# A six-stage decoder on one core: the constants of the last layers signalled in two parts, and ScalarE's copy of the second batch's first rows put ahead of the first rectifications

## The chip, the cores and the metric

The kernel runs on one core of one Trainium2 chip, in one launch. The metric is the time of one execution on the device in microseconds (us), the lower the better; a number given for a kernel is the median of several executions. The profiler records one execution apart from these.

The engines have short names in what follows: PE is TensorE (matrix products), ACT is ScalarE, DVE is VectorE, POOL is GpSimd, SP is SyncE (here it only issues transfers).

## The reference, cut to what matters

Eight batches of 256 rows with 256 columns pass through six layers. The change lies in the fourth, at its very start:

```python
x = _layernorm(x + _L0_attn_ref(...))      # attention over 16 heads
x = _layernorm(x + _L0_xattn_ref(...))     # attention over the context
x = _layernorm(x + _L0_ffn_ref(...))       # 8 experts, the best 2 of each row
x = _layernorm(x + _L1_attn_ref(...))      # gated attention and an MLP: the change is here
x = _layernorm(x + _L1_xattn_ref(...))
x = _layernorm(x + _L1_ffn_ref(...))

def _L1_attn_ref(x, ...):
    xn = _layernorm(x, ln1_g, ln1_b)
    q, k, v = l2norm(xn @ Wq), l2norm(xn @ Wk), xn @ Wv
    clock = softplus(xn @ clock_w + clock_b)
    gj = -softplus(xn @ gate_w + gate_b)
    gcp = exp(clip(cumsum(gj), -60, 50))
    p = xn @ p_w + p_b
    p_exp = exp(p - max(p)) * clock
    q = rope(q) * gcp / (cumsum(p_exp) + 1e-8)
    k = rope(k) / (gcp + 1e-8) * p_exp
    out = softmax(causal(q k^T / sqrt(Dh))) @ v @ out_w + out_b
    ...                                    # residual, layer norm, MLP with gelu
```

The cumulative sums run along the 256 rows of a batch, so a batch's gates, clocks and p have to be there whole before its scores.

## The kernel before, in words

The first three layers run as phases of their own and end at about 743 us of the span. The last three layers (the function the diff touches) then work on the eight batches in four groups of two batches (`G` groups, `GB` = 2 batches each). A group has four row tiles of 128 rows (`NT` = 4): tiles 0 and 1 are its first batch, tiles 2 and 3 its second (`HALF` = 2). The four groups pass through a pipeline of periods, with one group in its gated attention, the one before it in the rest of that layer, and one in the last layers. Before the pipeline is full there is a prologue for group 0 alone, done batch by batch. The change touches this prologue.

Each engine has its own program, written out in code in the order in which it runs; engines meet at semaphores. No planner or scheduler moves anything. The prologue's steps, with the names and lines of the kernel:

- POOL `gather(0)` (L1488) fetches the experts' results by eight indirect transfers; DVE `combine` (L2619) adds them to x. DVE `front_half` takes the statistics of a batch's two tiles, POOL `front_rstd` (L1532) raises them to a power, DVE `front_rows_of` (L2777) normalises tile by tile (`n3.normed` counts the tiles).
- ACT `front_rows(g, b)` (L2240) scales a normalised tile into `xn`, for two tiles of batch b (`n4.normed` counts). PE `turn` (L1640) transposes the two tiles into a bank, ACT `front_turned` (L2201) copies them out with gain and bias into `xnt`.
- PE `first_form(b, i)` (L1631), i from 0 to 5, forms the six products of a batch (two parts each of gate, clock and p) in two banks in turn. Form i waits until ACT has read form i-2 (`fmread`). ACT reads forms 0 to 3 in `first_rectified` (L2309 a Relu, L2310 an Abs, which signals `fmread`) and forms 4 and 5 in `first_p_rows` (L2316).
- ACT builds the softplus of gates and clocks from exponentials and logarithms (L2327, L2330, L2331, L2334, L2335), whose bias operands are the constants `ones` and `tiny`. DVE's scans (L2799, L2828) make the cumulative sums.
- PE `queries_keys` and `values` (L1631 too) make q, k and v; ACT `square` (L2266) and `value_copy` (L2271) read them. `value_copy` writes into `va`, which must have been filled with 0 and 1 before.

POOL fills the constants in `constants()`: `ones`, `tiny`, `mask1`, `maskx` and a column of `x5t` (L1500 to L1504). Then it waits until DVE has normalised all four tiles (`n3.normed` at `NT`), clears `va` (L1506), drains, writes a column of ones into it (L1508), cuts the two masks to triangles (L1509, L1511), drains again, and signals all of it by one semaphore, `const`.

Who waits for `const`: ACT, ahead of `first_forms(0)`; DVE, ahead of `first_gate(0)`; PE, ahead of `values(0, 0)`.

ACT's order in the prologue is: `front_rows(0, 0)`, `front_turned(0, 0)`, the wait for `const`, `first_forms(0)`, `front_turned(0, 1)`, `first_rows(0)`, and so on. Inside `first_forms(0)`, after the rectifications of forms 0 and 1, stands `front_rows(0, 1)`: the copy of the second batch's tiles. PE's order is: transposes of batch 0, forms 0 and 1 of batch 0, transposes of batch 1 (they need that copy), forms 2 to 5 of batch 0, and then `queries_keys` and `values`.

Of the kernel before, what the change touches and what calls it, by code (L numbers as in the profile page):

```python
# [45 lines left out]
class Memory:  # L46
# [14 lines left out]
    def sem(self, name):  # L61

        s = self.free.pop() if self.free else self.ctx.enter_context(self.nc.semaphore(name))
        self.used.append(s)
        return s
# [1233 lines left out]
def last_layers(nc, dram, memory, keep):  # L1299


    with ExitStack() as ctx:
# [3 lines left out]
        sem = memory.sem  # L1306
# [51 lines left out]
        lastxr, lastxk, lastrl, lastrs = (cut(gating, 1024 * i, dims) for i, dims in enumerate(((KD, GT), (KD, GT), (KD, GT), (NT, D))))  # L1358

        early, rows = keep["early"], keep["rows"]  # L1360
        weights, loaded, const, stored = (sem(f"l_{n}") for n in ("weights", "loaded", "const", "stored"))
        backed = [sem(f"backed{n}") for n in range(2 * NT)]
        fmm, fmread, qkmm, sqd, vmm, vcop = (sem(n) for n in ("fmm", "fmread", "qkmm", "sqd", "vmm", "vcop"))
        lgate, clr, gcr, ginv, uready, clogged, pmaxed, pexp, sumr, lsum, qsum, qfr, kfr = (sem(n) for n in (
# [29 lines left out]
        def x(g, t):  # L1394

            return keep["x"][:, NT * g + t, :]
# [9 lines left out]
        def batch(b):  # L1406

            return slice(b * S, (b + 1) * S)
# [5 lines left out]
        def tiles_of(b):  # L1414

            return slice(0, NT) if b is None else slice(HALF * b, HALF * b + HALF)

        def front_count(g, b):

            return 2 * g + (b or 0) + 1 if g < 2 else g + 3  # L1420
# [9 lines left out]
        def squares_of(g):  # L1430

            return (NT + 1) * g + 1 if g else 0

        def qk_bank(g, t):

            return (FIRSTQK if g == 0 else QKBANK)[t]
# [44 lines left out]
        def _(pool):  # L1481
# [16 lines left out]
            def constants():  # L1498

                pool.memset(ones[:, :], 1.0)  # L1500
                pool.memset(tiny[:, :], 1e-8)
                pool.memset(mask1[:, :], 3e38)
                pool.memset(maskx[:, :], 0.0)
                pool.memset(x5t[:, :, :, 0:1], 0.0)  # L1504
                pool.wait_ge(n3.normed, NT)
                pool.memset(va[:, :, :, :], 0.0)  # L1506
                pool.drain()
                pool.memset(va[:, :, :, DH1:DH1 + 1], 1.0)  # L1508
                pool.affine_select(out=mask1[:, :], in_=mask1[:, :], compare_op=ALU.is_ge,  # L1509
                                   fill=-1e30, base=0, pattern=[[1, P]], channel_multiplier=-1)  # L1510
                pool.affine_select(out=maskx[:, :], in_=maskx[:, :], compare_op=ALU.is_ge, fill=-8e13, base=0,  # L1511
                                   pattern=[[-1, S2]], channel_multiplier=1)
                pool.drain()
                pool.nop().then_inc(const, 1)
# [19 lines left out]
            front_rstd(0, 0)  # L1534
            front_rstd(0, 1)
            constants()
            pool.wait_ge(rows, NR * 16)
            for b in range(GB):
# [647 lines left out]
        def _(act):  # L2186
# [48 lines left out]
            def front_rows(g, b=None):  # L2235

                for t in range(NT)[tiles_of(b)]:
                    act.wait_ge(n3.rstd, front_count(g, t // HALF))
                    act.wait_ge(n3.normed, NT * g + t + 1)
                    act.activation(xn[:, t, :], x(g, t), ACT.Copy, scale=n4.inv[:, t:t + 1]).then_inc(n4.normed, 1)  # L2240
# [20 lines left out]
            def square(g, t):  # L2261

                act.wait_ge(qkmm, NT * g + t + 1)
                if t >= 2:
                    act.wait_ge(ssready, squares_of(g) + t - 1)
                act.activation((sq if g else firstsq)[:, t % 2, :], bank[qk_bank(g, t)][:, :], ACT.Square).then_inc(sqd, 1)  # L2266

            def value_copy(g, t):

                act.wait_ge(vmm, NT * g + t + 1)  # L2270
                act.activation(va[:, t, :, 0:DH1], bank[4 + t % 2][:, 0:D].rearrange("p (h d) -> p h d", d=DH1),  # L2271
                               ACT.Copy).then_inc(vcop, 1)
# [31 lines left out]
            def first_rectified(b, i, positive, size):  # L2304

                c = FORMS[i]
                bias = cols[:, (BP, BCLK, BGATE)[c // 2], c % 2:c % 2 + 1]
                act.wait_ge(fmm, 6 * b + i + 1)
                act.activation(positive[:, c % 2, batch(b)], bank[4 + i % 2][:, 0:S], ACT.Relu, bias=bias)  # L2309
                act.activation(size[:, c % 2, batch(b)], bank[4 + i % 2][:, 0:S], ACT.Abs, bias=bias).then_inc(fmread, 1)  # L2310

            def first_p_rows(b, i):

                c = FORMS[i]
                act.wait_ge(fmm, 6 * b + i + 1)
                act.activation(pexps[:, c, batch(b)], bank[4 + i % 2][:, 0:S], ACT.Identity, bias=cols[:, BP, c:c + 1]).then_inc(fmread, 1)  # L2316

            def first_forms(b):

                part = batch(b)  # L2320
                first_rectified(b, 0, gsum, gabs)
                first_rectified(b, 1, gsum, gabs)
                if b == 0:
                    front_rows(0, 1)
                first_rectified(b, 2, csum, cabs)
                act.drain()
                act.activation(gabs[:, :, part], gabs[:, :, part], ACT.Exp, scale=-1.0)  # L2327
                first_rectified(b, 3, csum, cabs)
                act.drain()
                act.activation(gabs[:, :, part], gabs[:, :, part], ACT.Ln, bias=ones[:, 0:1]).then_inc(lgate, 1)  # L2330
                act.activation(cabs[:, :, part], cabs[:, :, part], ACT.Exp, scale=-1.0)  # L2331
                first_p_rows(b, 4)
                act.drain()
                act.activation(qfac[:, :, part], cabs[:, :, part], ACT.Identity, bias=ones[:, 0:1])  # L2334
                act.activation(clog[:, :, part], cabs[:, :, part], ACT.Ln, bias=ones[:, 0:1]).then_inc(uready, 1)  # L2335
                first_p_rows(b, 5)

            def first_rows(b):

                square(0, HALF * b)  # L2340
                value_copy(0, HALF * b)
                value_copy(0, HALF * b + 1)
                act.wait_ge(pmaxed, b + 1)
                for c in range(KD):
                    last = act.activation(pexps[:, c, batch(b)], pexps[:, c, batch(b)], ACT.Exp, bias=pmax[:, GB * c + b:GB * c + b + 1])
                last.then_inc(pexp, 1)
                square(0, HALF * b + 1)
# [20 lines left out]
                act.wait_ge(qsum, b + 1)  # L2368
                act.activation(qfac[:, :, part], qfac[:, :, part], ACT.Exp, scale=-1.0).then_inc(qfr, 1)

            act.wait_ge(const, 1)
            first_forms(0)
            front_turned(0, 1)
            first_rows(0)
            first_gate(0)
            first_forms(1)
            first_factors(0)
            first_rows(1)
            first_gate(1)
            for j in range(PAIRS1):  # L2380
# [737 lines left out]
def decoder(nc, dram):  # L3118
    with ExitStack() as ctx:
# [28 lines left out]
        memory.free = keep["cleared"]  # L3148
        memory.mark = last
        last_layers(nc, dram, memory, keep)  # L3150


# [59 lines left out]
```

## Time and profile before

| what | value |
|---|---|
| time, median of 3 runs | 1292.72 us (1290.24, 1292.72, 1295.18) |
| the profiled execution's own time | 1288.51 us |
| its span, first to last instruction | 1286.8 us |
| PE busy | 1123.6 us, 87% of the span |
| DVE busy | 743.7 us, 58% |
| ACT busy | 544.2 us, 42% |
| POOL busy | 459.7 us, 36% |
| mean granted TensorE clock | 0.949 of full speed |

The share of PE is an average. In the prologue of the last layers PE is idle for long stretches, and what counts there is the chain of waits between the engines. A row of a timeline gives the start of a piece and its length in us, the engine, the line, what is written and read, how many instructions are merged in it, and in brackets how long the engine had been idle and who ended that. An "x2" piece is two instructions one behind the other. The engine name with a small q (POOLq, ACTq) is that engine's sequencer: drains and waits.

### The profile page before, as it was taken

To read this page: it belongs to the slowest core of one execution; us is meant where nothing else is said; L and a number is where in the kernel's file an instruction comes from. 1 tells how busy PE (TensorE), PEld (TensorE's weight loads), DVE (VectorE), ACT (ScalarE), POOL (GpSimd) and SP (SyncE) were. 2 spreads that over 40 slices of the span, in tenths; PEclk is the share of its full clock that TensorE was granted. 3 is DMA by queue.
4 is the path that set the end of the run, shared out by engine and by line. 5 is a ranking of instruction groups with operands and counts; after the bars stand their busy time and mean duration, and the time that the engine had idled before them with its cause. 6 is when DMAs were issued, how large, how long until landed. Compare 5 with 4: busy or idle time off the path is not lost. (4 is left out here: it accounts for less than half of the span.)

```text
span 1286.8 us, 20425 instructions
## 1 busy us (share of the span) xinstructions
PE 1123.6 (87%) x6750; PEld 796.0 (62%) x6750; DVE 743.7 (58%) x2260; ACT 544.2 (42%) x1407; POOL 459.7 (36%) x539
## 2 busy tenths in 40 slices
PE   7889988998899797799999937788898899789996
PEld 3466455644654576799999924454655575466775
DVE  1473367247534855455555637758748576856366
ACT  1371246125521741333333317466465457543541
POOL 0251025004400784566666541424221522222122
PEclk9999999999999998899999959689998999899999
DMA  5000010020001013741111141101000100000000
GB/s 194 17 1 1 28 46 2 1 56 17 1 1 56 2 55 124 266 145 48 45 50 51 42 141 39 33 1 29 5 8 1 34 9 17 1 1 25 1 1 33
DMA packets 40228, 52.38 MB, mean 41 GB/s; under 512 B 10780, under 2 KB 33372, under 8 KB 40124
## 3 DMA queue, kind: packets, MB, share of 16 engines
q1 hardware_dynamic: 31100, 36.66, 8.8%
q0 software_dynamic: 3408, 9.31, 2.6%
q10 hardware_dynamic: 5616, 5.11, 1.2%
q8 instruction: 55, 0.90, 0.3%
q14 instruction: 49, 0.40, 0.1%
HBM read 41.76 MB, written 9.31 MB: 40 GB/s over the span
## 5 line engine op out<-in xcount | busy, mean ns | idle before, releaser
L1631 PE MATMUL bank<-words 128*128 128x256 f32 (+3 forms) x872 | 276.1, 469 | 26.7 <-DVE words L2639 9.1
L1631 PEld LDWEIGHTS bank<-words 128*128 128x128 f32 (+1 forms) x872 | 166.7, 198 | 112.7 <-issue 58.0
L419 PE MATMUL bank<-words 128*128 128x512 f32 x384 | 171.6, 598 | 8.2 <-DMA words<-in_wq 8.2
L371 POOL TENSOR_TENSOR words<-words 128x256 f32<-128x256 f32 (+1 forms) x128 | 103.6, 831 | 176.3 <-DVE words L972 176.3
L1182 PEld LDWEIGHTS bank<-words 128*128 128x128 f32 x1248 | 147.4, 194 | 3.5 <-ACT words L1216 1.6
L1182 PE MATMUL bank<-words 128*128 128x128 f32 x1248 | 147.9, 277 | 0.9 <-ACT words L1216 0.9
L754 ACT ACTIVATE words<-words 128x128 f32<-128x128 f32 (+1 forms) x256 | 113.3, 444 | 52.8 <-DVE words L967 52.8
L419 PEld LDWEIGHTS bank<-words 128*128 128x128 f32 x384 | 72.1, 192 | 89.5 <-issue 88.9
L706 ACT ACTIVATE words<-bank 128x512 f32<-128x512 f32 x48 | 28.7, 598 | 191.0 <-PE bank L419 191.0
L1231 ACT ACTIVATE words<-words 128x1024 f32 x39 | 41.1, 1057 | 144.4 <-PE bank L1182 127.9
L808 DVE COPY words<-bank 128x512 f32<-128x512 f32 x48 | 33.2, 691 | 104.6 <-PE bank L419 104.3
L963 DVE CUSTOM_DVE_ANT_0 words<-bank,words 128x128 f32<-128x128 f32 (+1 forms) x256 | 76.0, 353 | 21.9 <-PE bank L430 20.6
L1193 PE MATMUL bank<-words 128*128 x312 | 73.9, 380 | 0.7 <-DVE words L1280 0.7
L443 PE MATMUL bank<-words 128*128 128x128 f32 x384 | 56.5, 285 | 16.0 <-POOL words L371 7.5
L430 PE MATMUL bank<-words 64*128 64x128 f32 (+1 forms) x512 | 60.4, 358 | 8.6 <-DVE words L967 5.2
L443 PEld LDWEIGHTS bank<-words 128*128 128x128 f32 x384 | 42.3, 144 | 37.6 <-issue 26.4
L456 PE MATMUL bank<-words 128*64 128x256 f32 (+1 forms) x512 | 56.4, 340 | 10.0 <-ACT words L762 9.0
L1524 POOL TENSOR_TENSOR words<-words 128x2 f32<-128x2 f32 x32 | 7.0, 218 | 162.0 <-DVE words L2649 161.9
L983 DVE COPY words<-bank 128x768 f32<-128x768 f32 x64 | 59.7, 932 | 7.6 <-PE bank L443 7.6
L2289 ACT ACTIVATE words<-bank 128x768 f32<-128x768 f32 x64 | 48.9, 811 | 31.8 <-DVE bank L2741 31.8
L1138 POOL COPY words<-words 128x1024 f32 x39 | 40.4, 1037 | 61.5 <-PE bank L1182 61.5
L2741 DVE TENSOR_TENSOR bank<-bank,words 128x512 f32<-128x512 f32 x64 | 42.0, 694 | 32.9 <-PE bank L1686 32.6
(346 smaller groups left out, 2013.6 us busy)
## 6 DMA issues: line engine op xcount, KB each, us to landing
words<-in_w SPq DMA_DIRECT2D x8, 1024.0 KB, 9.7
y_slots<-words ACTq DMA_DIRECT2D x39, 128.0 KB, 1.7
words<-in_w SPq DMA_DIRECT2D x8, 512.0 KB, 10.1
words<-in_xt SPq DMA_DIRECT2D x4, 512.0 KB, 3.8
words<-in_x SPq DMA_DIRECT2D x4, 512.0 KB, 4.1
x_rows<-words SPq DMA_DIRECT2D x16, 128.0 KB, 1.8
words<-in_wm SPq DMA_DIRECT2D x2, 1024.0 KB, 6.9
out_x<-words SPq DMA_DIRECT2D x16, 128.0 KB, 1.8
```

What stands on the lines that cost most here:

```text
L371: last = pool.tensor_tensor(part, part, inv[:, j % SLOTS0, :, t:t + 1].to_broadcast([P, 2, P * (t + 1)]), ALU.mult)
L419: last = pe.matmul(bank[c % 2][:, :], w, r, start=k == 0, stop=k == KD - 1)
L430: last = pe.matmul(bank[SCORES[i % 2][n]][:, t * P:t * P + P * (t + 1)],  kt[r, m, b * S + t * P:b * S + (t + 1) * P], qt[r, m, b * S:b * ...
L443: last = pe.transpose(bank[2 + n][:, k * P:(k + 1) * P], prob[:, j % SLOTS0, n, c:c + P], ident[:, :])
L456: last = pe.matmul(bank[4 + j % 2][DH0 * n:DH0 * n + DH0, queries], v[:, 2 * b + k, h * DH0:(h + 1) * DH0], probt[:, j % 2, n, probs_of], ...
L754: last = act.activation(prob[:, i % SLOTS0, n, c], prob[:, i % SLOTS0, n, c], ACT.Exp, bias=negmax[:, i % SLOTS0, n, t:t + 1], scale=DH0 * ...
L963: dve.tensor_tensor_reduce(out=prob[:, i % SLOTS0, n, c], in0=bank[SCORES[i % 2][n]][:, c], in1=mask0[:, c], scale=1.0, scalar=-3e38, op0= ...
L983: dve.tensor_copy(probt[:, j % 2, :, :], turned).then_inc(tcopied, 1)
L1182: last = pe.matmul(bank[(BANKG, BANKV)[half][j % 2]][:, c * P:(c + 1) * P], wfix[:, j % 2, k * 2 * FF + half * FF + c * P:k * 2 * FF + hal ...
L1193: last = pe.matmul(bank[BANKY[j % 2]][:, 0:D], hidden[:, j % 2, k * P:(k + 1) * P], w2[:, bass.ds(e * W2 + k * D, D)], start=k == 0, stop= ...
L1631: last = pe.matmul(out, w, r, start=i == 0, stop=i == len(pairs) - 1)
L2289: act.activation(es[:, j % 4, :, :], pair(j % 2)[:, :, 0:CAUSAL], ACT.Exp, scale=DH1 ** -0.5).then_inc(s1e, 1)
```

## The change

There is a new semaphore, `biases`. POOL signals it right behind the first five fills, after a drain of its own, and goes on to the wait and the clearing of `va` as before; `const` is still signalled at the end. ACT waits for `biases` where it waited for `const`, ahead of `first_forms(0)`, and waits for `const` in `first_rows`, ahead of the first copy into `va`. ACT's copy of the second batch's tiles, `front_rows(0, 1)`, is taken out of `first_forms(0)` and put ahead of that wait. The programs of PE, DVE and SP stay as they are.

```diff
-        weights, loaded, const, stored = (sem(f"l_{n}") for n in ("weights", "loaded", "const", "stored"))
+        weights, loaded, const, stored, biases = (sem(f"l_{n}") for n in ("weights", "loaded", "const", "stored", "biases"))
...
                 pool.memset(maskx[:, :], 0.0)
                 pool.memset(x5t[:, :, :, 0:1], 0.0)
+                pool.drain()
+                pool.nop().then_inc(biases, 1)
                 pool.wait_ge(n3.normed, NT)
                 pool.memset(va[:, :, :, :], 0.0)
...
                 first_rectified(b, 0, gsum, gabs)
                 first_rectified(b, 1, gsum, gabs)
-                if b == 0:
-                    front_rows(0, 1)
                 first_rectified(b, 2, csum, cabs)
...
             def first_rows(b):
 
                 square(0, HALF * b)
+                act.wait_ge(const, 1)
                 value_copy(0, HALF * b)
                 value_copy(0, HALF * b + 1)
...
-            act.wait_ge(const, 1)
+            front_rows(0, 1)
+            act.wait_ge(biases, 1)
             first_forms(0)
             front_turned(0, 1)
             first_rows(0)
```

ACT's instructions at the start of the last layers, before. L2240 is a pair of row copies, L2201 the copy of the transposed first batch, L2309 and L2310 the two reads of a form:

```order
655 L2240 ACTIVATE words<-words 128x256 x2
656 L2201 ACTIVATE words<-bank,words 128x256 x2
657 L2309 ACTIVATE words<-bank,words 128x256
658 L2310 ACTIVATE words<-bank,words 128x256
659 L2309 ACTIVATE words<-bank,words 128x256
660 L2310 ACTIVATE words<-bank,words 128x256
661 L2240 ACTIVATE words<-words 128x256 x2
662 L2309 ACTIVATE words<-bank,words 128x256
663 L2310 ACTIVATE words<-bank,words 128x256
664 L2327 ACTIVATE words<-words 128x2x256
```

And of the changed kernel, where the same lines are numbered two higher up to this place (L2242, L2203, L2311, L2312):

```order
655 L2242 ACTIVATE words<-words 128x256 x2
656 L2203 ACTIVATE words<-bank,words 128x256 x2
657 L2242 ACTIVATE words<-words 128x256 x2
658 L2311 ACTIVATE words<-bank,words 128x256
659 L2312 ACTIVATE words<-bank,words 128x256
660 L2311 ACTIVATE words<-bank,words 128x256
661 L2312 ACTIVATE words<-bank,words 128x256
662 L2311 ACTIVATE words<-bank,words 128x256
663 L2312 ACTIVATE words<-bank,words 128x256
664 L2327 ACTIVATE words<-words 128x2x256
```

The second pair of row copies has moved from behind the fourth read of a form to ahead of the first. Nothing else has moved, and ACT executes the same instructions as before.

## Rows read from the trace of the kernel before

**Rows 1.** Timeline of ACT, 759 to 780 us.

```profile
759.78 1.02 ACT L2201 ACTIVATE words<-bank,words 128x256 f32<-128x256 f32 x2 [0.87 <-PE bank L1640]
767.24 0.47 ACT L2309 ACTIVATE words<-bank,words 128x256 f32<-128x256 f32 x1 [6.44 <-POOLq L1513]
767.61 0.47 ACT L2310 ACTIVATE words<-bank,words 128x256 f32<-128x256 f32 x1
768.68 0.92 ACT L2240 ACTIVATE words<-words 128x256 f32<-128x256 f32 x2
772.12 0.47 ACT L2309 ACTIVATE words<-bank,words 128x256 f32<-128x256 f32 x1 [2.51 <-PE bank L1631]
773.58 0.46 ACT L2309 ACTIVATE words<-bank,words 128x256 f32<-128x256 f32 x1
779.15 0.39 ACT L2271 ACTIVATE words<-bank 128x256 f32<-128x256 f32 x1
```

**Rows 2.** Timeline of POOL, 763 to 778 us.

```profile
763.26 0.10 POOL L1504 MEMSET words<- 128x4 f32 x1
763.88 1.81 POOL L1506 MEMSET words<- 128x2048 f32 x1 [0.52 <-DVE words L2777]
777.66 1.28 POOL L1540 TENSOR_TENSOR words<-words 128x512 f32<-128x512 f32 x1 [10.51 <-ACT words L2335]
```

**Rows 3.** Chain of waits, 763 to 768 us: start, us, what.

```profile
763.36 0.51 issue
763.87 1.82 POOLq L1507
765.69 0.79 issue
...
766.90 0.32 POOLq L1513
```

**Rows 4.** Timeline of PE, 758 to 805 us and at 841 us.

```profile
760.85 3.78 PE L1631 MATMUL bank<-words 128*128 128x256 f32 x8 [1.11 <-ACT words L2201]
769.26 1.11 PE L1640 MATMUL bank<-words 128*128 128x128 f32 x4 [4.63 <-ACT words L2240]
770.17 3.97 PE L1631 MATMUL bank<-words 128*128 128x256 f32 x12
...
777.92 5.44 PE L1631 MATMUL bank<-words 128*128 128x256 f32 x20 [0.62 <-ACT words L2316]
...
792.02 3.71 PE L1631 MATMUL bank<-words 128*128 128x256 f32 x12 [0.62 <-ACT words L2316]
...
798.86 0.95 PE L1686 MATMUL bank<-words 32*128 32x256 f32 x16 [2.26 <-DVE words L2678]
801.43 2.35 PE L1686 MATMUL bank<-words 32*128 32x256 f32 x16 [1.61 <-ACT words L2289]
...
841.36 1.12 PE L1640 MATMUL bank<-words 128*128 128x128 f32 x4 [3.00 <-ACT words L2240]
```

**Rows 5.** Timeline of DVE, 762 to 797 us.

```profile
762.78 1.05 DVE L2777 TENSOR_SCALAR words<-words 128x256 f32<-128x256 f32 x2 [1.13 <-POOL words L1532]
775.31 1.27 DVE L2799 TENSOR_TENSOR_SCAN words<-words 128x256 f32<-128x256 f32 x2 [11.49 <-ACT words L2330]
```

**Rows 6.** Stretches: window, length, PE busy (instructions), granted clock, DMA share, GB/s.

```profile
758.00:764.60 6.60, 4.84 (x12) 0.50 0.26 66
764.60:769.20 4.60, 0.03 (x1) 0.50 1.04 388
769.20:772.40 3.20, 3.14 (x10) 0.50 1.10 348
772.40:799.90 27.50, 21.53 (x92) 1.00 0.14 41
799.90:806.50 6.60, 5.07 (x46) 0.50 0.00 0
```

**Rows 7.** The last of ten weight loads: its issue, and its way to landing.

```profile
768.77 0.72 SPq L1453 DMA_DIRECT2D words<-in_wv  x1
...
words<-in_wv SPq DMA_DIRECT2D x1, 256.0 KB, 7.3
```

## What the change does to the time: the prediction

> **What bounds the kernel now.** I first read the page's busy shares (PE 87% of the span) and then left them: the change touches one place, so the question is what ends last there. The timeline of ACT shows the place at once. ACT finishes copying the transposed first batch at 760.80 us (759.78 + 1.02) and then stands idle for 6.44 us, until POOL's last drain of the constants lets it go at 767.24 [rows 1]. The timeline of PE shows the harm: PE does its eight matmuls of forms 0 and 1 from 760.85 to 764.63, stands idle for 4.63 us, and goes on at 769.26 with the transposes of the second batch, released by ACT's row copy L2240 [rows 4]. That copy stood behind four reads of forms, which stood behind the wait for `const`. DVE is idle for 11.49 us in the same stretch [rows 5], and POOL itself for 10.51 us afterwards [rows 2]. So three engines wait in one chain that begins at POOL's fills, and the chain of waits of the whole program runs through it [rows 3]: nothing else covers this stretch. Time won here should be won at the end.
>
> **The sum, step by step.** All of it is in the times of the profiled execution.
>
> *The row copies.* DVE has normalised the second batch's last tile at 763.83 (762.78 + 1.05) [rows 5]. A pair of row copies takes 0.92 us on ACT, one of them about 0.5 [rows 1]. ACT, idle since 760.80, copies the first tile as soon as DVE gives it, and the second from about 763.95 to 764.47. PE ends form 1 at 764.63 [rows 4], so the copies are there when PE comes to its transposes, and they wait for nothing. That is the main term: PE's idle time of 4.63 us before the transposes goes to about 0.
>
> *The new signal.* POOL's fifth fill ends at 763.36 (763.26 + 0.10) [rows 2]. The new drain and signal have no row of their own. The nearest rows bound them: the drain after the small instructions took 0.32 us, the one after the large fill was followed by another 0.79 us of issue [rows 3]. The signal itself is quick: ACT went on 0.02 us after the last drain's end (767.22 to 767.24), so the lower bound is about 0. The upper is 0.79. So `biases` comes between 763.4 and 764.2, and ACT is busy with the copies until 764.47. I take 0 for it: the copies hide it. Without that cover each further tenth would count only after a slack that I work out next.
>
> *The first reads of forms.* Form 0 has long been ready at 762.8 (half of the eight matmuls). ACT reads it from 764.4, with 0.37 us from start to start and 0.47 us for one [rows 1], so the signal that the first bank is free comes at about 765.25. PE needs it after the transposes, whose start to the next matmul's start is 0.91 us (770.17 - 769.26) [rows 4]: 764.63 + 0.91 = 765.54. There are 0.3 us to spare. ACT ends its fourth read at about 765.95, well before form 2 is ready.
>
> *Form 2.* Before, ACT began to read it at 772.12 [rows 1], which is 1.95 us after PE began it at 770.17. After: 765.54 + 1.95 = 767.49. So ACT's chain through the softplus, DVE's scans, the squares and the keys is moved up by 4.63 us.
>
> *What is late next.* `const` now comes later on POOL, since the drain stands ahead of the large fill: by nothing up to (763.36 + 0.32 + 0.79 - 763.88 =) 0.6 us, so at 767.2 to 767.8. The first to need it is DVE's scan, before at 775.31 [rows 5], after at 770.7; that leaves 2.9 us. ACT's first copy into `va` comes at 779.15 - 4.63 = 774.5 [rows 1], and PE's values, which follow the last read of a form at 777.92 [rows 4], at about 773.3. The added waits cost nothing there: what is queued behind them never sees them. POOL's next work waits for ACT [rows 2] and moves up with it. The two waits are semaphore waits that are already met, 0 us each, at most some hundredths.
>
> *Transfers.* The ten weight loads are issued by SP after statistics that do not move. The last one is issued at 768.77 and takes about 7.3 us [rows 7], to 776.8. PE needs them only in the first period, after work at 841.36 that waits for ACT [rows 4]; nothing there turns into a new wait. The stretch in which they are loaded at 388 GB/s [rows 6] will now hold the forms' matmuls, but the forms at 770 to 772 already ran under 348 GB/s with matmuls of the same length as those at 761.
>
> *The clock.* The granted clock is at its lower level (0.50, 1.2 GHz) from 758 to 772.40, then at the higher (2.4 GHz) until 799.90 [rows 6]. It rose after PE had been busy for 3.1 us; PE's idle stretch of 4.60 us lay before that. Eight matmuls took 3.78 us at the lower level, 0.47 each. The twelve from 770.17 took 3.97, of which the first four, at the lower level, took about 1.9, and the other eight about 0.26 each. Two ends follow. If the clock is up when form 2 begins, form 2 takes 1.1 us and not 1.95: 0.8 us more gain. If it rises only after form 3, form 3 ends at 767.44 + 1.9 = 769.3, while ACT would want it at 773.58 - 4.63 = 768.95 [rows 1]: 0.4 us less gain. Between -0.4 and +0.8 I take 0, a rise while form 2 or 3 runs.
>
> The Trainium skill ("TensorE: Matmul & The Clock Gate", Part 1) says that the array is throttled by default, that sustained activity releases it, and that the moment isn't tied to the kernel's start, so that it differs from run to run. The trace agrees with the first part: the low level lasted through an idle stretch and ended after one of busy work [rows 6]. The second part one execution cannot show; by it both ends above would occur in different executions, and the sum stays.
>
> *Sum.* 4.63 + 0 + 0 + 0 = 4.6 us, own range 4.2 to 5.5. The profiled execution would go from 1288.51 to 1283.9 (its span from 1286.8 to 1282.2). It lies 4.2 us under the median of the runs, so for the median I take the difference: 1292.72 - 4.6 = 1288.1. That is 0.36%. About 0.5% (6.5 us, so below 1286.3 or above 1299.2) is what a measurement of this kernel can tell from no change; the three runs alone span 4.9 us.
>
> **The rivals.**
>
> *A, the half gain: the new signal does not come early.* If POOL's signal came as late as `const` does now (the drain waiting for more than the small fills), ACT would have the copies done but read form 0 at 767.24. PE would do the transposes at 764.63, then wait for the free bank until 767.61 + 0.47 = 768.08; form 2 would end at 770.03. ACT's read of it would move from 772.12 to 770.0: a gain of 2.1 us, 1290.6. Against it: the drains in the rows took tenths, and the large fill comes only behind the signal.
>
> *B, more than the forecast: the clock.* The clock falls at 799.90, and the pairs of score matmuls (L1686, x16) that took 0.95 us at the higher level took 2.35 at the lower [rows 4]. If the level is up for form 2 (0.8 us) and one more such pair on the path is still done at the higher level (1.4 us), the gain is 4.6 + 0.8 + 1.4 = 6.8 us: 1285.9, which is faster by more than 0.5%. For it: the whole prologue comes 4.6 us earlier relative to the last fall, and the busy stretch is unbroken. Against it: the same shift can as well put a pair under the lower level.
>
> *C, on the other side: the clock stays low through the forms.* The busy stretch at 758 to 764.6 did not raise it [rows 6]. If from 764.6 on it stays at the lower level until the scores, the work from 777.92 (eight matmuls of 256 columns and four of 512 up to ACT's second square, 3.7 us of the 5.44) takes 16 x 0.47 = 7.5, +3.8; the form that ACT waits for in the second batch +0.8; form 3 +0.4; and the last twelve from 792.02, 3.71 us [rows 4], take 7.5 too and come onto the path, about +3.5. Together 8.5 us against 4.6: slower by 3.9, 1296.6. It decides from the point where the level stays low past the twelve matmuls. Against it: the stretch gets denser for PE, and a less dense one raised the clock.
>
> *D, the gain is hidden anyway*: some later wait for a transfer or an engine that has not moved takes it. Then 1292.7. In the rows I find no such fixed point before 841 us: the weights are early by 60 us.
>
> **How the numbers follow.** Forecast 0.76, A 0.07, B 0.10, C 0.03, D 0.04. The time is the forecast's, 1288.1. The range goes from 1283.5 (below B, with some of the runs' scatter) to 1293.0 (D and A inside, C left out). Faster by over 0.5%: B, and the part of the forecast that the scatter of medians carries past 1286.3, together 0.22. Slower by over 0.5%: even C doesn't reach 1299.2, 0.02 is left for what I haven't seen. Within 0.5%: 0.76.
>
> **What would show it.** In the changed kernel's profile: PE's idle time before the second batch's transposes near 0 (if 1 us or more, the row copies are late); ACT's third read of a form about 2 us behind PE's start of form 2, and near 767.5 on the old scale; ACT's first read released near 764.4 and not by POOL (if POOL's sequencer is named and the time is past 764.7, the signal is dear; near 767, A); the large fill at 763.9 to 764.5; no wait on `const` in front of DVE's first scan or the first copy into `va`; the distance from the end of form 1 to the first period shorter by 4.6 us. A rise of the clock while form 2 or 3 runs would bear out the middle of my clock term; a rise after the second batch's forms is C. I am wrong in the main thing if PE's gap closes and the distance to the first period doesn't shrink by 4 us or more.

## The result: 4 to 5 us faster, and the profile after

Timed right after the prediction, the changed kernel took 1285.78 us (median of 5 runs, 1284.86 to 1286.86) and the kernel before 1290.90 (5 runs). The two kernels were compared three times:

| comparison | kernel before | changed kernel | ratio | 95% interval |
|---|---|---|---|---|
| first | 1290.90 (5 runs) | 1285.78 (5) | 0.9953 | 0.9936 to 0.9971 |
| second | 1290.94 (35) | 1287.97 (12) | 0.9979 | 0.9966 to 0.9992 |
| third | 1290.69 (25) | 1286.32 (10) | 0.9956 | 0.9940 to 0.9972 |
| control: before against itself, twice | | | 1.0002 and 0.9999 | 0.9990 to 1.0014; 0.9985 to 1.0012 |

The plain mean of the three ratios is 0.9963, or 4.8 us of 1291. A ratio is worked out from all runs and is not the quotient of the two medians beside it; by the medians alone the gains are 5.1, 3.0 and 4.4 us, 4.2 in the mean. The forecast was a gain of 4.6 us and 1288.1 us; the measured 1285.78 lies in the stated range. Of the 2.3 us between them 1.8 come from the kernel before, whose median was 1292.72 of three runs when the forecast was made and is 1290.90 of five. All three ratios lie within 0.5% of 1, as forecast for the likeliest case, though the first interval and the third reach beyond it. The profiled execution took 1286.09 us of its own.

In the changed kernel's numbering L2242 are the row copies (L2240 before), L2203 the copy of the transposed batch, L2311 and L2312 the reads of a form, L1633 the products and L1642 the transposes. First its timeline of ACT, the answer to [rows 1]:

```profile
758.06 1.02 ACT L2203 ACTIVATE words<-bank,words 128x256 f32<-128x256 f32 x2 [0.87 <-PE bank L1642]
761.88 0.91 ACT L2242 ACTIVATE words<-words 128x256 f32<-128x256 f32 x2 [2.81 <-DVE words L2779]
762.70 0.46 ACT L2311 ACTIVATE words<-bank,words 128x256 f32<-128x256 f32 x1
763.05 0.46 ACT L2312 ACTIVATE words<-bank,words 128x256 f32<-128x256 f32 x1
...
765.49 0.48 ACT L2311 ACTIVATE words<-bank,words 128x256 f32<-128x256 f32 x1 [1.24 <-PE bank L1633]
...
766.95 0.46 ACT L2311 ACTIVATE words<-bank,words 128x256 f32<-128x256 f32 x1
...
772.52 0.39 ACT L2273 ACTIVATE words<-bank 128x256 f32<-128x256 f32 x1
```

The wait of 6.44 us for POOL is gone. ACT now waits 2.81 us for DVE's normalised rows, copies them, and reads form 0 right behind that without any idle time. The timeline of PE, to [rows 4]:

```profile
759.13 3.78 PE L1633 MATMUL bank<-words 128*128 128x256 f32 x8 [1.11 <-ACT words L2203]
762.70 1.06 PE L1642 MATMUL bank<-words 128*128 128x128 f32 x4
763.57 3.94 PE L1633 MATMUL bank<-words 128*128 128x256 f32 x12
...
771.29 5.44 PE L1633 MATMUL bank<-words 128*128 128x256 f32 x20 [0.62 <-ACT words L2318]
...
792.23 1.56 PE L1688 MATMUL bank<-words 32*128 32x256 f32 x16 [2.25 <-DVE words L2680]
```

No idle time stands ahead of the transposes at 762.70, where there were 4.63 us. This execution had started form 0 1.72 us earlier than the one before (759.13 against 760.85), which is scatter of what lies ahead. So from here on places are compared by their distance from PE's start of form 0: the transposes moved from 8.41 to 3.57, form 2 from 9.32 to 4.44, the first scores of batch 0 (L1688, L1686 before) from 38.01 to 33.10.

POOL and DVE, to [rows 2] and [rows 5]:

```profile
761.54 0.10 POOL L1504 MEMSET words<- 128x4 f32 x1
762.47 1.81 POOL L1508 MEMSET words<- 128x2048 f32 x1 [0.83 <-DVE words L2779]
764.41 0.20 POOL L1510 MEMSET words<- 128x64 f32 x1
...
764.78 0.28 POOL L1513 TENSOR_SCALAR_AFFINE_SELECT words<-words 128x120 f32<-128x120 f32 x1
```

```profile
761.05 1.05 DVE L2779 TENSOR_SCALAR words<-words 128x256 f32<-128x256 f32 x2 [1.13 <-POOL words L1534]
...
768.69 1.27 DVE L2801 TENSOR_TENSOR_SCAN words<-words 128x256 f32<-128x256 f32 x2 [6.58 <-ACT words L2330]
```

The large fill starts 0.3 us later by the distance from form 0 (3.34 for 3.03), but only 0.13 us lie between its end and the next fill, where there were 0.80. The last cut of a mask ends at 5.93 us after form 0, before at 6.29. DVE's scan comes at 9.56 instead of 14.46, still released by ACT.

The stretches, to [rows 6] (window, length, PE busy and instructions, granted clock, DMA share, GB/s):

```profile
757.00:762.70 5.70, 4.59 (x12) 0.50 0.26 77
762.70:765.90 3.20, 3.20 (x12) 0.62 1.02 390
765.90:793.00 27.10, 21.16 (x82) 0.99 0.33 102
```

The clock is at the lower level (1.2 GHz) in the first stretch, in which PE is busy for 4.6 of 5.7 us, and rises to the higher one (2.4 GHz) in the unbroken busy stretch behind it. By its mean of 0.62 it was up for 0.24 of that stretch, so from about 765.1, 6.0 us after form 0 and late in form 2. Before, the higher level was there from 772.40, 11.5 us after form 0.

### The profile page after: what moved, and what is told of

Read it like the earlier page. It is cut to its first block and busy times, and to the rows that moved or that the text cites. A ratio compares the mean times of both kernels' runs of the same rounds, so it can differ in the third digit from the quotient of the medians.

```text
span 1284.4 us, 20428 instructions
## 1 busy us (share of the span) xinstructions
PE 1123.9 (88%) x6750; PEld 796.4 (62%) x6750; DVE 742.0 (58%) x2260; ACT 543.6 (42%) x1407; POOL 459.0 (36%) x539
## 5 line engine op out<-in xcount | busy, mean ns | idle before, releaser
L1633 PE MATMUL bank<-words 128*128 128x256 f32 (+3 forms) x872 | 276.0, 468 | 27.1 <-DVE words L2641 9.1
L1633 PEld LDWEIGHTS bank<-words 128*128 128x128 f32 (+1 forms) x872 | 166.5, 198 | 113.2 <-issue 58.1
```

The source lines that it names most:

```text
L1633: last = pe.matmul(out, w, r, start=i == 0, stop=i == len(pairs) - 1)
```

## The experiments

**Three more traces of each of the two kernels, unaltered** (twice with times and once with a profile alone). The changed kernel again:

> The changed kernel once more, unaltered, for a second trace and a second set of times. In its first trace the distance from PE's form 0 to the first scores of batch 0 was 33.1 us (before: 38.0), but from form 0 to the first scores of batch 1 59.1 us (before: 60.3): 3 us of the gain were lost where DVE waits twice for 1.5 to 2.2 us ahead of the keys of batch 1 (L2677), while POOL issues the indirect transfers. Theory 'scatter of that one execution': in this trace the distance to batch 1's scores is about 56 us, the gain of 4.3 to 4.9 us stays whole, and the times lie 4.5 to 5.5 us under the kernel before. Rival 'part of the change': the two waits are here again, the distance is 59 us again, and the times lie 1 to 2 us under the kernel before unless something elsewhere pays for it.

The kernel before again:

> The kernel before once more, unaltered, for a second trace and for the measurement's own error. Both theories expect a ratio of 1.000 within 0.2%. Its first profiled execution took 1288.51 us, 1.7 us less than its fastest timed run. Theory 'scatter': this trace has again 38.0 us from form 0 to the scores of batch 0, and its own time is nearer to the timed runs' median of 1291. Rival 'the change's loss at batch 1 is real and something else in the timed runs hides it': again 60.3 us from form 0 to batch 1's scores, without the two DVE waits.

Third traces:

> The kernel before, a third trace, for how often DVE waits ahead of batch 1's keys. If the wait is the usual thing, PE's idle time before batch 1's first scores is 4.6 to 4.9 us and form 0 to these scores 63 to 64 us; if it comes in half of the executions either 60.3 or 63.7. The distance from form 0 to batch 0's scores is 38.0 us in either case.

> The changed kernel, a third trace. Form 0 to the first scores of batch 0 is 32.3 to 33.1 us again, by whether the TensorE clock rises before or after form 2; PE does not idle before the second batch's transposes (under 0.1 us). Form 0 to batch 1's scores is 57.7 to 59.1 us with DVE's wait and 55 to 56 without.

And fourth traces, with times:

> The kernel before, timed beside it in as many runs, so that the two can be set against each other without the label's effect. Both theories expect a ratio of 1.000 within 0.15%, and 83.6 or 86.9 us from form 0 to the first division of the first period.

> The changed kernel, timed once more against the kernel before, to settle how much of the local gain reaches the end. In the traces so far the distance from form 0 to the first division of the first period (L2713 of before) is 83.6 and 83.8 us before and 77.9 after where DVE does not wait ahead of batch 1's keys, 86.9 before and 80.8 and 82.6 after where it does: 4.3 to 6.1 us of gain, 5.3 in the mean. Theory 'the gain stays whole': ratio 0.9955 to 0.9970, that is 4 to 5.5 us. Rival 'the periods give some back': 0.9975 to 0.9985, 2 to 3 us. Trace: 32.3 to 33.1 us from form 0 to batch 0's scores.

Measured, in us after PE's start of form 0. The first division of the first period is the next fixed point after the prologue; "DVE waits" is whether DVE stood 3.5 to 3.7 us in all ahead of batch 1's keys, where 0.7 is the least seen.

| trace | own time | batch 0's scores | DVE waits | batch 1's scores | first division | end |
|---|---|---|---|---|---|---|
| before, first | 1288.51 | 38.01 | no | 60.31 | 83.83 | 525.95 |
| before_3 | 1282.18 | 38.01 | no | 60.35 | 83.55 | 521.95 |
| again_before | 1295.39 | 38.03 | yes | 63.74 | 86.89 | 531.60 |
| before_4 | 1292.91 | 38.03 | yes | 63.65 | 86.69 | 531.28 |
| changed, first | 1286.09 | 33.10 | yes | 59.07 | 82.58 | 525.27 |
| again_after | 1286.17 | 32.33 | yes | 57.66 | 80.80 | 524.30 |
| after_4 | 1287.69 | 32.34 | yes | 57.76 | 80.53 | 523.68 |
| after_3 | 1278.48 | 32.35 | no | 54.68 | 77.88 | 517.58 |

The local gain is steady: 4.9 us at batch 0's scores in the first trace and 5.7 in the other three. At the first division it is 5.7 to 6.0 us between traces that both lack the wait, and 4.1 to 6.4 between those that both have it. At the end it is 4.4 to 8.4 without and 6.0 to 7.9 with, so the periods scatter by several us, but don't give the gain back.

The table also separates the two things that disturb a comparison of single traces. From batch 0's first scores to batch 1's it takes 22.3 us in the three traces without the wait, of either kernel (22.30, 22.34, 22.33), and 25.3 to 26.0 in the five with it. The spread of these five is the clock's: batch 0's first 16 score matmuls took 1.56 us in the changed kernel's first trace, 1.29 in again_before, 1.17 in before_4 and 0.95 in all others, and with their surplus taken off the five lie from 25.3 to 25.4. So this stretch passes the gain on whole, and the wait adds 3.0 to 3.1 us to either kernel.

The times say somewhat less, 2.7 to 6.1 us by the three ratios. Only the second comparison is lower than expected (the expectation said 4.5 to 5.5 us if the wait was mere scatter): its interval goes from 1.0 to 4.4 us and leaves out the 4.6 of the forecast. The third, at 5.7 us, lies where its expectation put it if the gain stays whole (0.9955 to 0.9970). How much of the local gain is lost by the end, if any, these times don't settle. Of my two theories for the lost 3 us of the first trace, neither was right as put. The wait is not a part of the change, since the kernel before has it too; and it is not scatter from one execution to the next either, as the last section tells.

**Only the signal in two parts.**

```diff
                 first_rectified(b, 1, gsum, gabs)
+                if b == 0:
+                    front_rows(0, 1)
                 first_rectified(b, 2, csum, cabs)
...
-            front_rows(0, 1)
             act.wait_ge(biases, 1)
```

> Only the signal in two parts: ACT waits for biases ahead of the first forms and for const ahead of the first copy into va, but the second batch's row copies stay behind four reads of forms. My theory: ACT reads form 0 at once (2.3 to 3 us after PE's start of form 0) and form 1 when PE ends it (3.8 us after), the row copies follow at 4.7 us, PE's transposes start at about 5.1 us after form 0 and not 8.4 as before or 3.6 as with both parts. PE's idle time before them is 1.3 us; gain 3.2 to 3.5 us in the distance from form 0 to batch 0's scores (34.6 us), time 3.3 us under the kernel before. Rival 'the move is the change': the signal comes late (after POOL's drain, 1 us or more past the last small fill) and the gain is under 1.5 us.

The diff is against the changed kernel. Timeline of ACT and of PE in this kernel (here and below a piece that the window's edge cuts is shown with the matmuls inside the window alone):

```profile
766.32 0.47 ACT L2311 ACTIVATE words<-bank,words 128x256 f32<-128x256 f32 x1 [3.32 <-POOLq L1505]
...
767.76 0.92 ACT L2242 ACTIVATE words<-words 128x256 f32<-128x256 f32 x2
```

```profile
763.05 3.78 PE L1633 MATMUL bank<-words 128*128 128x256 f32 x8 [1.11 <-ACT words L2203]
768.33 0.84 PE L1642 MATMUL bank<-words 128*128 128x128 f32 x4 [1.50 <-ACT words L2242]
```

PE idles for 1.50 us (1.3 expected) and transposes 5.28 us after form 0 (5.1 expected); form 2 begins at 5.96. Batch 0's scores come at 33.76 where 34.6 were expected; the difference is an earlier rise of the clock, whose granted value is 1.00 already from 768.30 to 769.10, 5.3 us after form 0. This run also prices the new signal, which the changed kernel hides. Its chain of waits reads:

```profile
763.90 2.40 POOLq L1505
766.29 0.02 issue
766.32 0.47 ACT words L2311
```

The last small fill ended at 765.56 (765.46 + 0.10), POOL's new drain at 766.29 or 766.30: the drain and the signal cost 0.73 to 0.76 us, and `biases` comes 3.27 us after form 0. That is later than the 2.3 to 3 us I had expected of the reading, and near the upper of my two bounds. Time: 1288.87 us, ratio 0.9987 (0.9975 to 1.0000), 1.7 us by the ratio where 3.3 were expected and 4.3 stand in the trace, so this expectation was missed. In the same comparison the changed kernel had only 0.9979.

**Only the move.**

```diff
                 first_rectified(b, 1, gsum, gabs)
-                if b == 0:
-                    front_rows(0, 1)
                 first_rectified(b, 2, csum, cabs)
...
+            front_rows(0, 1)
             act.wait_ge(const, 1)
             first_forms(0)
```

> Only the move: the second batch's row copies stand ahead of the wait, which is still for const in one part. My theory: the copies are done when PE ends form 1, PE transposes without idle time, but form 2 must wait until ACT, let go by const 6.4 us after PE's start of form 0, has read form 0 (7.2 us after). PE idles for 2.6 us there instead, form 2 begins 7.2 to 7.3 us after form 0 and not 9.3, and the gain is 2.0 to 2.2 us: 1288.8 if the kernel before is at 1290.9. Rival 'the move is all of it': the gain is over 4 us. Rival 'the move without the split is worth nothing': under 0.5 us.

The diff is against the kernel before. Timelines of ACT and PE:

```profile
762.85 0.91 ACT L2240 ACTIVATE words<-words 128x256 f32<-128x256 f32 x2 [2.80 <-DVE words L2776]
766.49 0.47 ACT L2309 ACTIVATE words<-bank,words 128x256 f32<-128x256 f32 x1 [2.72 <-POOLq L1513]
```

```profile
760.10 3.78 PE L1631 MATMUL bank<-words 128*128 128x256 f32 x8 [1.11 <-ACT words L2201]
763.68 0.92 PE L1640 MATMUL bank<-words 128*128 128x128 f32 x4
767.38 3.05 PE L1631 MATMUL bank<-words 128*128 128x256 f32 x7 [2.78 <-ACT words L2310]
```

Form 2 begins 7.28 us after form 0, as expected to the tenth. PE transposes early, and then idles for 2.78 us until `const` lets ACT free a bank. Batch 0's scores come at 36.08, 1.9 us sooner than before. Time: 1289.13 us, ratio 0.9987 (0.9973 to 1.0001), 1.7 us where 2.0 to 2.2 were expected. The times can't tell the two parts from each other, and hardly from the kernel before; what each is worth rests on one trace each. At batch 0's scores the split alone gains 4.3 us, the move alone 1.9, both 4.9 to 5.7. In these numbers stands the clock's rise, which differs from trace to trace; at the start of form 2 they are 3.4, 2.0 and 4.9 us. Neither part does it alone.

**The first signal late.** POOL gives `biases` only after it has cleared `va`:

```diff
-                pool.drain()
-                pool.nop().then_inc(biases, 1)
                 pool.wait_ge(n3.normed, NT)
                 pool.memset(va[:, :, :, :], 0.0)
                 pool.drain()
+                pool.nop().then_inc(biases, 1)
```

> The changed kernel with the first signal late: POOL gives biases after it has cleared va and drained, and not ahead of that. ACT's row copies still stand in front. My reckoning of the slack: PE's transposes begin at 3.6 us after form 0 as now; the signal comes at 5.1 to 5.7 us, ACT ends its first two reads 0.84 us later, so PE begins form 2 at 6.0 to 6.6 us instead of 4.4 and the distance to batch 0's scores is 34.0 to 35.2 us instead of 32.3 to 33.1. So every us of the signal beyond some 4.0 us after form 0 would count in full. Rival 'the signal has more slack than 0.3 us': under 1 us is lost.

Timelines of ACT and PE:

```profile
766.96 0.47 ACT L2310 ACTIVATE words<-bank,words 128x256 f32<-128x256 f32 x1 [1.94 <-POOLq L1507]
```

```profile
761.36 3.78 PE L1632 MATMUL bank<-words 128*128 128x256 f32 x8 [1.11 <-ACT words L2202]
...
767.85 2.50 PE L1632 MATMUL bank<-words 128*128 128x256 f32 x5 [1.85 <-ACT words L2311]
```

The signal takes effect 5.60 us after form 0 and form 2 begins at 6.49, both in the range expected. Batch 0's scores come at 35.62, 0.4 us past the upper end that I gave. Of the 2.5 us against the changed kernel's first trace, 2.05 are form 2's delay. The rest goes with the clock, which was at the lower level all through forms 2 and 3 (granted clock 0.50 from 767.85 to 773.00): ACT's third and fourth pairs of reads stand 2.11 and 3.81 us after form 2's start, 1.92 and 3.38 in the changed kernel. The chain from the signal to form 2 is thus as reckoned, but its slack was not: the signal took effect 2.03 us later than ACT's first read in the changed kernel (5.60 for 3.57) and form 2 began 2.05 later. So once the signal is later than the row copies, at 3.6 us and not at 4.0, its delay counts in full. This is one execution, without a set of times.

**The clock up before the forms.**

```diff
+            pe.wait_ge(n3.stats, 1)
+            for _ in range(12):
+                pe.matmul(bank[7][:, 0:P], ident[:, :], ident[:, :], start=True, stop=True)
             turn(0, n4, 0, lambda t: xn[:, t, :], bank[2])
```

> The changed kernel, and PE does twelve needless 128x128 products into a free bank once the first batch's statistics are there (about 3 us ahead of its first transposes), so that its clock may be up when the forms begin. They change nothing in the result. Theory 'the clock sets the last 0.8 us': the granted clock is 1.00 for most of forms 0 and 1, which then take 2.1 to 2.8 us and not 3.8; PE then waits for the row copies at about 3.5 us after its first form, since these do not depend on it, and the distance from form 0 to batch 0's scores is 32.3 us or up to 0.5 us more or less, never the 33.1 of the first trace. Time 0 to 1 us under after_4, which these runs can hardly tell. Rival 'the clock is no part of it': 33.1 us or more, or the products come in the way of the first transposes and the time is over 1 us longer.

Timeline of PE:

```profile
757.83 5.37 PE L1838 MATMUL bank<-words 128*128 128x128 f32 x24 [12.92 <-issue]
763.04 0.60 PE L1642 MATMUL bank<-words 128*128 128x128 f32 x4
764.75 1.99 PE L1633 MATMUL bank<-words 128*128 128x256 f32 x8 [1.11 <-ACT words L2206]
766.59 0.60 PE L1642 MATMUL bank<-words 128*128 128x128 f32 x4
767.38 3.19 PE L1633 MATMUL bank<-words 128*128 128x256 f32 x12 [0.19 <-ACT words L2315]
```

The clock was up (granted 1.00 from 764.75 on): the eight matmuls took 1.99 us and not 3.78. But each product became two instructions, 24 in 5.37 us, and they stood in the way of the first transposes, so form 0 started 4.66 us after the first row copy (760.09) and not 2.85, 1.8 us late. Nothing was lost by that and nothing won: DVE's normalising of the second batch began at 764.86 in this trace and batch 0's scores at 795.30, 30.44 us after it; in after_4 it is 794.66 - 764.24 = 30.42. Form 2 began 2.52 us after DVE's start in this trace and 2.51 in after_4, both times released by ACT's read of form 0. In the changed kernel's first trace, where the clock rose late in form 2, DVE's rows to the scores took 31.18 us: that is the clock's 0.8 us, measured from a point that PE does not move. Time: 1286.12 us, ratio 0.9960 (0.9944 to 0.9975), the same as after_4's 0.9956. So with the clock up in time, forms 0 and 1 are no longer the bound: form 2 waits for the chain of DVE's normalised rows, ACT's copies of them and ACT's first reads. My expectation was wrong in two points. PE did not idle ahead of the second batch's transposes, but 0.19 us behind them, and the distance from form 0 to the scores was 30.55 us and not 32.3, since form 0 itself came late. That it would gain nothing if form 0 were on time follows from these rows, but was not run.

**The next group's transfers later**, to rid batch 1 of DVE's wait:

```diff
             pool.wait_ge(vmm, NT)
+            pool.wait_ge(qkt, NT)
             gather(1)
```

> The changed kernel, and POOL waits for the last keys of batch 1 (qkt at 4) before it issues the eight indirect transfers of group 1's rows. In five of the six traces so far, before and after alike, DVE waits 2.9 to 3.7 us ahead of those keys (L2675 or L2677, released by 'remote') while POOL issues these transfers, and PE is idle for 4.6 to 4.9 us before batch 1's first scores; in the first trace of the kernel before that was 1.6 us. Theory 'POOL's indirect transfers hold DVE up there': the wait is gone, PE idles 1.6 us before batch 1's first scores, the distance from form 0 to them falls from 57.7 to 59.1 down to 54.6 to 56 us; of these 3 us up to 2 may be paid back where DVE waits for the rows; time 1 to 3 us under again_after. Rival 'the wait is not the transfers' but comes from PE's or DVE's own supply': PE's idle time stays at 4.6 us or more and the time does not fall.

> The kernel before with the same later transfers and nothing else. Theory 'transfers': batch 1's first scores at 60.3 us after form 0 (as in the one trace without the DVE wait), not 63.7. If the change and the wait are independent, late_gather is faster than this one by the whole 4.9 us that the change wins locally, 0.38%. Rival 'the change's net gain is smaller than its local one because something else gives way': the two differ by 2 to 3.5 us only, as the two kernels did in the second measurement (ratio 0.9979).

These two ran together with before_3 and after_3, and none of the four traces has the wait, with or without the edit. So they can't tell what causes it. They do tell the price of the edit: DVE now waits for the rows, in late_gather:

```profile
818.71 0.48 DVE L2622 SCALAR_TENSOR_TENSOR words<-words 128x256 f32<-128x256 f32 x1 [1.50 <-DMA words<-y_slots,words]
...
821.21 0.48 DVE L2622 SCALAR_TENSOR_TENSOR words<-words 128x256 f32<-128x256 f32 x1 [1.41 <-DMA words<-y_slots,words]
```

There are four such waits, and the first division comes at 81.63 us instead of after_3's 77.88. Times: late_gather 1285.62 us, ratio 0.9988 (0.9969 to 1.0007); late_gather_before 1290.80, ratio 1.0024 (1.0002 to 1.0047); the kernel before had 1287.00 here. The quotient of the two, 0.9964, is the change once more with the transfers late: 4.6 us, though their intervals together leave anything from about 1 to 8. In their traces the first division comes 5.8 us sooner with the change (81.63 for 87.43), as in the pairs without this edit. No version beat the changed kernel clearly.

## Why the prediction was right, point by point

*PE's idle time before the transposes.* Predicted 4.63 us to 0: right. The transposes moved by 4.84 us, because in an unbroken stream they start 0.2 us before the modelled end of form 1; the idle time in the timeline is a little less than what a filled gap gives back.

*Row copies in time.* Predicted to end at 3.62 us after form 0 (764.47), measured 3.66 (762.79). They are just in time. In the run with the clock up, form 2 waited for them and for ACT's first reads behind them, and not for form 1.

*The new signal.* Predicted to cost nothing, within 0 to 0.79 us after the last small fill. Measured in split_only 0.73 to 0.76, near the upper end; it is hidden by the copies with 0.30 us to spare (3.27 against 3.57).

*The bank release.* I gave it 0.3 us of slack. There is none: the transposes' earlier start used up 0.2, and where the clock rises during them PE waits for it, 0.28 us in after_3:

```profile
762.61 0.67 PE L1642 MATMUL bank<-words 128*128 128x128 f32 x4
763.56 1.99 PE L1633 MATMUL bank<-words 128*128 128x256 f32 x8 [0.28 <-ACT words L2312]
```

ACT's release itself came at 4.4 us after form 0, as reckoned.

*`const` later.* Predicted 0 to 0.6 us later with 2.9 us to spare. It came about 0.4 us earlier. The step was wrong in sign and without effect, since nobody waits for it.

*The clock.* The term was 0, between -0.4 and +0.8. The gain measured at batch 0's scores is 4.9 us in the first trace, where the level rose when form 2 was nearly done, and 5.7 in the other three. There all of form 2 ran at the higher level (twelve matmuls in 3.19 us and not 3.94). Against the 4.84 us of the transposes that is +0.1 and +0.8. The upper end was right in size and occurred in three traces of four, the lower one did not occur, and this is the term of the sum that was mis-sized: with the 0.2 us of the transposes it makes the forecast's 4.6 us into 5.5 locally, in the mean of four traces. That the gain in the times, 4.2 to 4.8 us, lies nearer to the forecast than the local one does is no merit of the sum: nothing in it foresaw a loss on the way, and the times are too rough to show one. The Trainium skill ("TensorE: Matmul & The Clock Gate", Part 1) says that the moment of the rise isn't tied to the kernel's start. Here that is borne out: it came 3.4 us after form 0 in after_3, 4.3 in again_after and 6.0 in the first trace, by the granted clock of their stretches (0.98 from 762.50 to 763.00, 0.60 from 763.60 to 764.60, and 0.62 as shown above).

*Nothing else late.* Right: no new wait on transfers or on `const` stands in any trace of the changed kernel, and the first period's start moves with the prologue.

*The rivals.* A, the late signal, is refuted by the first trace, and the run move_only gives its price as reckoned (form 2 at 7.28 us after form 0, against 7.23 in the text). B, the clock's further gain, came true in its first part (0.8 us), not in its second: the second pair of score matmuls took 2.35 us in all eight traces. B took the fall of the clock for a fixed point that the prologue moves away from, and it is none. It fell 38.9 us after form 0 before the change (about 799.7, by a granted clock of 0.76 from 799.50 to 799.90) and 33.3 us after it in the changed kernel's first trace (about 792.4, by 0.93 from 792.00 to 792.50 and 0.50 behind that), so it came forward with the work, and there by more than the scores did. That the measured 1285.78 is B's 1285.9 is chance. C did not occur in any. D is refuted by the traces and by the ratios.

## What to carry to other kernels

When one signal covers several constants, look at who waits for which of them: here an engine stood 6.4 us for a fill that it needed 12 us later. Then follow what is queued behind the wait on the same engine, because about a third of the worth lay in a small copy behind it that another engine wanted: at form 2's start the split alone gained 3.4 us, the two together 4.9. And before reading two single profiles against each other, take each again: the first pair here would have shown 1.3 us of gain at the first period where like pairs show 4.1 to 6.4.

## What was not expected of the hardware

DVE sometimes waits 3.5 to 3.7 us, 3 us longer than else, ahead of batch 1's keys, while POOL issues indirect transfers. In again_before PE's last transposes of these keys had ended by 821.15, 2 us before DVE went on, and the profile names no engine of the core for the wait ("remote"). The timeline of DVE in again_before, and then in before_3:

```profile
818.34 1.33 DVE L2851 TENSOR_TENSOR words<-words 128x512 f32<-128x512 f32 x2
823.20 0.42 DVE L2675 TENSOR_TENSOR words<-bank,words 128x256 f32<-128x256 f32 x1 [3.53 <-remote]
```

```profile
814.37 1.31 DVE L2851 TENSOR_TENSOR words<-words 128x512 f32<-128x512 f32 x2
816.43 0.42 DVE L2675 TENSOR_TENSOR words<-bank,words 128x256 f32<-128x256 f32 x1 [0.74 <-PE bank L1831]
```

All eight traces of the second and third comparison have it, with either kernel, and none of the four that ran together (before_3, after_3 and the two with late transfers). In all eight a second wait of 2.6 to 3.3 us follows about 80 us later, over the end of the next series of such transfers. So it seems to belong to something that lasts for a whole series of runs, and not to the kernel. The first pair is split, the changed kernel with it and the kernel before without, and says nothing on that. In the series without the wait the kernel before had a median of 1287.00 us, in the two with it 1290.94 and 1290.69; single profiled executions follow this less well (without the wait 1282.18 and 1288.51, with it 1292.91 and 1295.39).

Where DVE goes on is telling. In seven of the nine traces with the wait that is 0.14 to 0.20 us after the end of the last of POOL's eight indirect transfers' issues (in again_before 823.20, for 822.11 + 0.95), in the other two, both of the changed kernel, 0.00 and 0.05 us after the end of the seventh. That fits POOL holding up DVE, but in before_3 DVE goes on at 816.43 in the middle of these issues, which last until 819.05. What differs between the series stays open.

The small drain with its signal cost POOL 0.73 to 0.76 us behind five short fills, but the drain behind the large fill then left only 0.13 us of gap where there had been 0.80, in the changed kernel (764.28 to 764.41). So it is in all 14 traces: 0.13 or 0.14 us in the seven with the early drain, 0.80 to 0.83 in the seven without, late_signal among them. The first of the drains pays, it seems, whatever stands before it. Why is open, and no run was made for it.
